# Third and fourth combined tiles later among the last expert's down tiles, a fold that starts after an input split, and the last result by hidden unit

## The reference

```
# layer 0
w_b = sum_g cond_8[b,g] * weight[g] * mask          # one 256x256 matrix per sequence
x = x + attention(x @ w_b.T + bias)                 # 2 heads of 128, causal, rotary on half of a head
h = gated MLP of the expert argmax(cond_8[b])(x)    # silu(up) * gate, down, with biases
x = x + routed_ffn(h)                               # 8 experts, 2 per token, 640 slots each, gelu gate
# layer 1
h = two picked gated MLPs (weighted) + shared MLP   # width 1024
x = x + minGRU scan over tokens(h)
x = x + ffn(base + LoRA(x))                         # ternary weights, width 1024, gelu
```

## Time and profile before

| what | value |
|---|---|
| median of 3 runs | 930.07 us (929.25 to 931.79) |
| the profiled execution, its own time | 926.78 us |
| its span, first to last instruction | 925.5 us |
| TensorE busy | 911.2 us (98% of the span) |
| VectorE busy | 528.7 us (57%) |
| ScalarE busy | 444.4 us (48%) |
| GpSimd busy | 269.8 us (29%) |
| chain that ended last, TensorE's share | 89% |
| mean granted TensorE clock | 1.000 |

### The profile page before, as it was taken

One profiled execution on the slowest core, in us unless ns is written; L12 is line 12 of the kernel. 1 busy time (PEld: TensorE's weight loads), 2 busy tenths in 40 slices (PEclk: granted clock), 3 DMA queues, 4 the chain that ended last, 5 costly groups with the idle time before them and its releaser, 6 DMA issues.

```text
span 925.5 us, 13114 instructions
## 1 busy us (share of the span) xinstructions
PE 911.2 (98%) x4859; PEld 767.9 (83%) x4859; DVE 528.7 (57%) x975; ACT 444.4 (48%) x827; POOL 269.8 (29%) x242
## 2 busy tenths in 40 slices
PE   8999999999999999999999999999999999999998
PEld 4768868887799999998888888888888888888886
DVE  6754454578757766785665564333333335688544
ACT  3665566434355455572343343343343442345775
POOL 1533321310475765653400152041140230010000
PEclk9999999999999999999999999999999999999999
DMA  8030001220445343432503013003003011000011
GB/s 301 30 114 23 24 1 69 104 81 28 121 129 157 125 126 126 126 125 77 180 18 148 12 24 137 0 1 137 1 8 129 1 55 83 1 0 1 1 46 46
DMA packets 22192, 67.47 MB, mean 73 GB/s; under 512 B 4514, under 2 KB 11954, under 8 KB 19314
## 3 DMA queue, kind: packets, MB, share of 16 engines
q1 hardware_dynamic: 16546, 40.15, 11.9%
q0 software_dynamic: 5440, 26.50, 9.9%
q10 hardware_dynamic: 144, 0.00, 0.0%
HBM read 55.09 MB, written 9.45 MB: 70 GB/s over the span
## 4 chain that ended last, share of the span: by engine, by line
PE 89%; DVE 4%; issue 2%; DMA 2%; ACT 2%; POOL 1%; SPq 0%; ACTq 0%; DVEq 0%; POOLq 0%
PE banks L1112 18%; PE banks L1114 18%; PE banks L1113 18%; PE banks L1365 5%; PE banks L1367 5%; PE banks L1366 5%; PE banks L1206 3%; PE banks L1190 3%; PE banks L1404 2%; PE banks L1403 2%; PE banks L1197 2%; PE banks L1417 1%; PE banks L1416 1%; PE banks L1160 1%; DMA weight_stage<-in_cond_w 1%
## 5 line engine op out<-in xcount | busy, mean ns | idle before, releaser
L1112 PE MATMUL banks<-input_hi,mlp_hi 128*128 128x512 f32 x376 | 147.6, 392 | 0.0
L1114 PE MATMUL banks<-input_hi,mlp_lo 128*128 128x512 f32 x376 | 146.4, 389 | 0.0
L1113 PE MATMUL banks<-input_lo,mlp_hi 128*128 128x512 f32 x376 | 146.4, 389 | 0.0
L1631 ACT CAST hidden_hi<-hidden 128x512 fp32r<-128x512 f32 x96 | 59.6, 621 | 158.6 <-DVE hidden L2048 107.5
L2237 POOL TENSOR_TENSOR mlp_lo<-weight_stage,mlp_hi 128x768 fp32r<-128x768 f32 x32 | 59.1, 1846 | 172.4 <-ACT mlp_hi L1609 172.4
L2054 DVE TENSOR_TENSOR hidden_lo<-hidden,hidden_hi 128x512 fp32r<-128x512 f32 x96 | 66.4, 692 | 61.7 <-ACT hidden_hi L1631 61.4
L2048 DVE SCALAR_TENSOR_TENSOR hidden<-banks,L_expert_weight,gelu 128x512 f32<-128x512 f32 x64 | 48.0, 750 | 83.6 <-PE banks L1114 80.5
L1625 ACT ACTIVATE gelu<-banks 128x512 f32<-128x512 f32 x96 | 57.4, 598 | 71.2 <-PE banks L1114 63.5
L1114 PEld LDWEIGHTS banks<-input_hi,mlp_lo 128*128 128x128 f32 x376 | 70.6, 188 | 14.8
L1113 PEld LDWEIGHTS banks<-input_lo,mlp_hi 128*128 128x128 f32 x376 | 70.6, 188 | 14.4
L1112 PEld LDWEIGHTS banks<-input_hi,mlp_hi 128*128 128x128 f32 x376 | 70.6, 188 | 14.2
(11 more groups left out here) (350 smaller groups left out, 2148.8 us busy)
## 6 DMA issues: line engine op xcount, KB each, us to landing
weight_stage<-in_packF SPq DMA_DIRECT2D x8, 1536.0 KB, 7.0
weight_stage<-in_shared SPq DMA_DIRECT2D x2, 3072.0 KB, 11.2
expert_output<-y_rows SPq DMA_DIRECT2D x40, 128.0 KB, 1.8
weight_stage<-in_cond_w SPq DMA_DIRECT2D x4, 512.0 KB, 5.3
residual<-in_xT SPq DMA_DIRECT2D x4, 512.0 KB, 10.7
first_half_swapped<-first_half SPq DMA_DIRECT2D x16, 128.0 KB, 2.0
routed_input<-x_rows SPq DMA_DIRECT2D x16, 128.0 KB, 1.7
weight_stage<-in_ffn_w SPq DMA_DIRECT2D x2, 1024.0 KB, 7.1
```

Source lines behind the costliest of these rows:

```text
L1112: pe.matmul(o, wh, dh, start=(i == 0), stop=False)
L1113: pe.matmul(o, wh, dl, start=False, stop=False)
L1114: last = pe.matmul(o, wl, dh, start=False, stop=(i == len(terms) - 1))
L1631: act.copy(hiD[n % 4][:, :], prod_t[n % 2][:, :]).then_inc(done)
```

## The change

Six edits:

1. Sequence 1's fold no longer takes two side steps ahead of the input split of chunk 2; the split comes first, all four folds behind it.
2. `inverse(last - 1)` moves from behind the second of the last chunk's down tiles to behind the fourth, just ahead of `inverse(last)`.
3. Beside the last expert, `comb` 2 moves from up step 6 to behind down tile 1, `yt` 2 from behind down tile 0 to behind down tile 2, `comb` 3 from behind down tile 1 to behind down tile 3, `yt` 3 from behind down tile 3 to behind down tile 4.
4. The last three hidden units' down products go unit by unit, both halves of each, and the two results behind all of them.
5. In the last chunk the running count is no longer updated (one VectorE instruction less).
6. SyncE's fetch of expert 2's weights also waits for `he_lo` of expert 0, second half, first unit.

```diff
@@ plan()
-    run(weave(attention(1), chain(some(fold, 2), later_input(2), fold, later_input(3), rotated("k", 2), rotated("q", 2), value_tiles(2))))
+    run(weave(attention(1), chain(later_input(2), fold, later_input(3), rotated("k", 2), rotated("q", 2), value_tiles(2))))
@@ all_chunks()
         for t in range(1, QT):
             down(last, t)
-            if t == 1:
-                inverse(last - 1)
             yield
+        inverse(last - 1)
         inverse(last)
@@ beside_last_expert()
-            if 4 <= step <= 6:
+            if 4 <= step <= 5:
                 dve.append(("comb", step - 4))
...
             yield
+        yield
+        dve.append(("comb", 2))
+        yield
         pe.append(("yt", 2))
         yield
         dve.append(("comb", 3))
-        yield
         yield
         pe.append(("yt", 3))
         yield
@@ end of plan()
+    for c, i in under_way[:-2]:
+        ffn_down(c, i)
+    before_last, last_unit = under_way[-2:]
+    for unit, k in ((before_last, 0), (before_last, 1), (last_unit, 0), (last_unit, 1)):
+        pe.append(("f2_of", *unit, k))
     for k in range(KD):
-        for c, i in under_way:
-            pe.append(("f2_of", c, i, k))
         dve.append(("result", NCH - 1, k))
@@ vector_program(), "pos"
-                step(dve.tensor_tensor(pos[:, :, :], o[:, 0:QT * G].rearrange("p (t e) -> p t e", e=G), cnt, ALU.add))
-                dve.tensor_tensor(counts[1 - c % 2][:, :], o[:, QT * G:(QT + 1) * G], counts[c % 2][:, :], ALU.add).then_inc(done)
+                placed = dve.tensor_tensor(pos[:, :, :], o[:, 0:QT * G].rearrange("p (t e) -> p t e", e=G), cnt, ALU.add)
+                if c < NCH - 1:
+                    step(placed)
+                    dve.tensor_tensor(counts[1 - c % 2][:, :], o[:, QT * G:(QT + 1) * G], counts[c % 2][:, :], ALU.add).then_inc(done)
+                else:
+                    placed.then_inc(done)
@@ sync_program()
                 sp.wait_ge(*(ready("wf_lo", e, 5) if e else ready("first_wf_lo", 5)))
+                if e == 0:
+                    sp.wait_ge(*ready("he_lo", 0, 1, 0))
                 fetch_expert(e + 2)
```

## The result

| kernel | median, us | executions | against before, 95% interval |
|---|---|---|---|
| before | 930.85 (929.25 to 932.46) | 6 | |
| changed | 935.56 (933.55 to 936.22) | 6 | 1.0048 (1.0033 to 1.0063) |

The changed kernel is slower by 0.48%, some 4.5 us. The profiled execution took 933.55 us with a span of 932.3 (before: 926.78 and 925.5). Its mean granted TensorE clock was 1.000; in the five others it was 0.996 (two) or 0.998 (three). That difference turns out to matter. (These are means over the whole span; what stretch they come from, only a trace tells.)

What follows compares the result with a forecast made beforehand. TensorE, busy 98% of the span, bounds the kernel, so only its idle time or a shorter end can gain. 2.82 - 0.30 + 0.59 - 0.43 = +2.7 us on the median 930.07 gives 932.8 us; range 931.0 to 936.0.

Steps and rivals of the forecast that it cites:

- the clock rival: TensorE's clock falls in the fold's new 3.9 us gap: up to another 2.5 us, 935.3 us; chance 0.27.
- the likeliest case: The forecast itself: +2.7 us, 932.8 us, own range 931.8 to 933.8; chance 0.55.
- 1, the fold: Sequence 1's second fold waits for `fold_lo`, TensorE idle 3.93 us; +2.82 us.
- 2, the inverse and the count: Last chunk: eight small `inverse(last - 1)` products move into the 1.5 us gap, -0.30 us; count instruction 0.
- 3, the combined tiles: Last expert's down tiles: stalls of 1.08 and 0.2 go, two of 1.0 come; +0.59 us.
- 4, the end: Last hidden units: no wait, `result` 1 0.54 earlier, 0.1 given back for stores that may meet; -0.43 us.
- 5, the fetch: Expert 2's weights, issued about 9.3 us later, land at 267.5, before first needed at 271.27; 0.
- The bank does not bind: Rival: second fold finds a free bank or early `fold_lo`; sum -1.2 us, 928.8 us; chance 0.11.
- Both new waits vanish: Rival: bank free and `comb` never late at the last expert; sum -3.5 us, 926.6 us; chance 0.07.
- The sum: Whole kernel: +2.7 us on the profiled 926.78, the same shift on the median 930.07 giving 932.8 us.

Runs made afterwards that it cites:

- fold_alone: The kernel before with only the fold's edit (input split first, all four folds behind it); 932.07 us against 927.30, ratio 1.0052.
- fold_again: The kernel before with only the fold's edit, run a second time, on the third chip; 935.27 us against 931.00, ratio 1.0045.
- fold_back: The changed kernel with the fold's edit undone and the other five edits kept; 927.13 us against 927.30 before, ratio 1.0000.
- two_tiles: The kernel before with the inverse, count and end edits and each `yt` two tiles behind its `comb`; 930.14 us against 931.35, ratio 0.9984.
- comb_alone: The kernel before with only the last expert's `comb` and `yt` edit; 927.97 us against 927.30, ratio 1.0012.
- one_fold_ahead: The kernel before with one fold ahead of the input split instead of two; 931.88 us against 931.35, ratio 1.0007.
- fold_hi_first: The kernel before with the fold's edit, first `fold_hi` ahead of the 768-wide `exp` and its `fold_lo` ahead of the `max`; 931.19 us against 931.35, ratio 1.0002.
- gap_full: The changed kernel with 17 spins (unread products) in the gap ahead of the second fold; 935.77 us against 931.35 before, ratio 1.0040.
- fold_fill7: The kernel before with only the fold's edit plus 7 spins (unread products) in the gap; 934.70 us against 931.00, ratio 1.0048.

## Why the prediction was right or wrong

The side was right (slower, 0.53). The range held 935.56 only because its upper end had been drawn out to hold the clock rival; the forecast's own range ended at 933.8. The number, 932.8, was 2.8 too low: 0.8 is that the kernel before came out at 930.85 and not 930.07, and 2.0 that the change added 4.7 and not 2.7, because the likeliest case was not the one that came. Part by part:

- **1, the fold.** Forecast 2.82 with 3.93 idle, counted from the spacing; the trace has 2.78 with 3.68, which is 3.85 with the tail of 0.17 that a bracket leaves out. Executions with the gap filled and without the edit, at full clock, differ by 2.75. Every link came where it was put: `x0_lo` 52.73, the start's 0.31 taken off 52.42 (forecast 52.45); `fold_lo` 56.31, 56.00 (56.03). No wait behind it gave anything back.
- **The step that failed** is the weighing of the first rival, the clock, at 0.27. Its argument against, that TensorE had never worked before the gap of 3.78 at the start, had nothing behind it. On the first chip, fold_alone had it below 1.000 in 5 of 5 executions and the kernel before in none of 23. Of all 19 executions with the 3.7 us gap (changed kernel, fold_alone, fold_again) 17 had it, but on the other chips some of these falls may sit in the expert stage. With the clock as the forecast the number would have been 935.3. Its price was given as up to 2.5; it is 2.0 in the medians of the first group, and 0, 1.6 and 2.8 in single traces. That the changed kernel's own executions lost it at the fold is inferred from this, since its one profiled execution had no fall. The Trainium skill, "TensorE: Matmul & The Clock Gate", section "Why this matters for your kernels", warns of just such a gap; the traces agree in the main, and its rule would have made the better forecast, though the changed kernel's own profiled execution took the gap without a fall.
- **2, the inverse and the count.** -0.30 forecast, -0.18 and, in fold_back, -0.15 measured. The eight small products take less out of the down tiles' path than the 0.41 less 0.11 of their row; that part was over-sized by 0.12 to 0.15.
- **3, the combined tiles.** +0.59 forecast; 0.66 in the changed kernel, 0.65 in fold_back. The chain, forecast at 2.48, measured 2.47 twice. The waits are 0.61 and 0.84, with the tail 0.78 and 1.01, against 1.0 forecast. With two tiles to hide in, in two_tiles, the chain costs nothing. "Could the chain be shorter? No" held; it can only be started earlier. What the sum did not ask is whether the late row holds TensorE in every execution: in three of seven traces with the old order it doesn't, and against those the same edit costs 1.7 to 2.1 us. On the first chip the medians still gave +0.7 (comb_alone).
- **4, the end.** -0.43 forecast, -0.43 measured, -0.49 in fold_back. The 0.1 given back for the stores was a guess and no run tested it alone.
- **5, the fetch.** 0 forecast, 0 in fold_back.
- **The other rivals.** "The bank does not bind" is out by the wait, though one_fold_ahead and fold_hi_first show that it binds only through the place of `fold_hi`. "Both new waits vanish" describes two_tiles at its `comb`, not the change.
- **The sum.** "A median 3.3 above the profiled execution, the same shift" was carried over without asking what the 3.3 were. They look like what two of the chips show (expert 0's first products, falls of the clock), and an execution may have them or not.

## What to carry to other kernels

When work is moved so that an engine waits, price the wait twice: once for its length, and once for TensorE's clock, which here made 2.8 us into 4.8 at a gap of 3.7 us. A shared bank is not late by itself; look at which long instruction stands ahead of its reader in the other engines' lists, and move the reader, as fold_hi_first did. A chain of fixed length (2.48 us here) is hidden by starting it early enough, so count the tiles between its start and its use before moving either end. And before pricing a wait from one trace, see in others whether it is there each time: the late row before `yt` 2 was in four of seven.

## What was not expected of the hardware

- The clock can fall behind a gap or inside it: in fold_alone it was 1.00 while TensorE idled, then 0.69 and 0.74; in fold_again and gap_full it fell before TensorE worked again (0.77 from 54 to 57 us, 0.90 from 183 to 186), so that all that followed at once was at half speed. Both folds' falls were over by 63 us. The same gap gave a loss of 0, 1.6 and 2.8 us in three profiled executions, so one profile doesn't settle whether a kernel pays it. A mean granted clock of 0.998 (fold_alone) or 0.996 (fold_again) over a span of 930 us is the trace of it.
- The length of the gap alone doesn't tell. One of 2.76 us brought a fall (gap_full), one of 2.17 none (fold_fill7); the 1.68 at expert 0 brought one in two_tiles, and 1.68 to 1.78 at the same place none in the seven other traces that have it. Gaps of 1.24 (fold_hi_first) and 1.3 us (the last `inverse`) brought none.
- The same 128x8 copy on VectorE took 0.17 us in the kernel before and 1.26 to 1.29 in two of four kernels with spins, ahead of a wait of TensorE of 0.37 that grew to 1.56 and 2.76. The cause is open.
- The kernel before had medians of 927.3, 931.35 and 931.0 us on three chips; the traces put the difference at the start of the experts (some 2.6 us for the same kernel) and in the clock. Comparisons across chips of less than that say nothing.
